# Moving the 8-head attention's value products to other PSUM banks and re-timing a four-layer kernel

## The reference

```python
x = L0(x)  # batchnorm, 3x3 depthwise + 1x1 conv to q,k,v; k,v resized to 7x7; 4-head attention with a bias;
           # 3x3 depthwise + 1x1 conv; + x; batchnorm, relu, 1x1 conv; + residue
x = L1(x)  # group norm; softmax(k) over channels, softmax(q) over pixels; k^T v; q (k^T v); 1x1 conv; + normed x
x = L2(x)  # group norm; qkv; 8 heads of 32 channels: softmax(q^T k / sqrt(32)) v; 1x1 conv; + x
x = L3(x)  # group norm; one head of 256 channels: softmax(q^T k / 16) v; 1x1 conv; + x
```

## Time and profile before

| what | value |
|---|---|
| median of 3 runs | 2110.89 us (2110.83 to 2111.57) |
| the profiled execution | 2112.12 us |
| its span, first to last instruction | 2109.7 us |
| mean granted TensorE clock | 0.98 |
| PE busy | 2011.4 us, 95% |
| ACT busy | 1886.4 us, 89% |
| DVE busy | 1843.0 us, 87% |
| POOL busy | 973.3 us, 46% |

### The profile page before, as it was taken

The page is one execution under the profiler, slowest core; times in us unless marked ns, Lnnn a source line. Parts: engine busy times, 40 slices in busy tenths (PEclk is TensorE's granted clock), DMA queues, the critical chain, the costliest instruction groups (busy, mean ns, idle before and its releaser), DMA issues.

```text
span 2109.7 us, 57712 instructions
## 1 busy us (share of the span) xinstructions
PE 2011.4 (95%) x15232; PEld 1689.6 (80%) x15232; DVE 1843.0 (87%) x4683; ACT 1886.4 (89%) x6231; POOL 973.3 (46%) x1707
## 2 busy tenths in 40 slices
PE   4589999999999999999999999999999999999977
PEld 3367888888888888888888888888888888888766
DVE  6789999999999999999999999999999999997532
ACT  2269999999999999999999999999999999999984
POOL 3544544545444454544445454444545544453211
PEclk8799999999999999999999999999999999999988
DMA  4000011001101100110111011011101101000000
GB/s 129 16 24 24 17 40 40 24 30 38 38 23 38 38 30 24 38 38 23 38 38 36 18 38 38 23 38 38 38 15 38 38 27 34 31 32 17 24 24 39
DMA packets 29819, 70.31 MB, mean 33 GB/s; under 512 B 6252, under 2 KB 7088, under 8 KB 29744
## 3 DMA queue, kind: packets, MB, share of 16 engines
q1 hardware_dynamic: 26928, 67.68, 9.1%
q10 hardware_dynamic: 2816, 1.72, 0.3%
HBM read 30.85 MB, written 12.85 MB: 21 GB/s over the span
## 4 chain that ended last, share of the span: by engine, by line
PE 88%; ACT 4%; DVE 1%; issue 1%; DVEq 0%; ACTq 0%
PE ps_e L1167 21%; PE ps_c L1167 21%; PE ps_b L1167 15%; PE ps_a L1167 11%; PE ps_s L1167 10%; PE ps_s L1222 8%; ACT e L830 1%; PE ps_a L1469 1%; ACT e L822 1%; ACT pt L836 0%; PE ps_e L1298 0%; PE ps_a L1298 0%; DVE nm L958 0%; ACT e L877 0%; ACT kv L742 0%
## 5 line engine op out<-in xcount | busy, mean ns | idle before, releaser
L822 ACT ACTIVATE e<-ps_s,nm 98x196 f32<-98x196 f32 x1024 | 423.9, 436 | 36.2 <-DVE nm L958 32.0
L830 ACT ACTIVATE e<-e,rden 98x196 f32<-98x196 f32 x1024 | 403.2, 462 | 0.2 <-DVE rden L1063 0.2
L1159 DVE SCALAR_TENSOR_TENSOR y<-opad,w_dw,y 128x406 f32<-128x406 f32 x512 | 314.9, 666 | 0.0
L1140 DVE SCALAR_TENSOR_TENSOR y<-xpad,w_dw,y 128x406 f32<-128x406 f32 x512 | 298.4, 636 | 0.0
L587 POOL TENSOR_SCALAR xn<-x,gn_scale,gn_shift 128x196 f32<-128x196 f32 x384 | 286.1, 757 | 20.8 <-POOL gn_shift L582 20.8
L575 POOL TENSOR_TENSOR gn_t<-gn_group 128x4 f32<-128x4 f32 x96 | 27.7, 289 | 563.7 <-DVE gn_group L1008 430.1
L958 DVE TENSOR_REDUCE nm<-ps_s 98x4 f32<-98x784 f32 x256 | 239.4, 966 | 34.2 <-PE ps_s L1167 34.2
L836 ACT COPY pt<-ps_s 98x392 f32<-98x392 f32 x512 | 233.3, 502 | 4.7 <-PE ps_s L1222 2.8
L1222 PE MATMUL ps_s<-w_eye,e 98*98 98x98 f32 x2048 | 228.9, 249 | 7.3 <-ACT e L830 7.2
L1222 PEld LDWEIGHTS ps_s<-w_eye,e 98*98 98x98 f32 x2048 | 200.5, 130 | 38.8 <-issue 22.3
L822 ACT ACTIVATION_READ_ACCUMULATOR e<-ps_s,nm 98x1 f32 x1024 | 222.7, 217 | 0.0
(11 more groups left out here) (223 smaller groups left out, 5326.6 us busy)
## 6 DMA issues: line engine op xcount, KB each, us to landing
x_in<-in_x SPq DMA_DIRECT2D x32, 392.0 KB, 3.2
x_res<-in_x SPq DMA_DIRECT2D x32, 392.0 KB, 3.1
x2b<-x SPq DMA_DIRECT2D x32, 392.0 KB, 2.7
out<-x SPq DMA_DIRECT2D x32, 392.0 KB, 2.6
out_pairs<-out SPq DMA_DIRECT2D x32, 392.0 KB, 2.5
w_q<-in_q SPq DMA_DIRECT2D x3, 256.0 KB
w_k<-in_k SPq DMA_DIRECT2D x3, 256.0 KB
w_v<-in_v SPq DMA_DIRECT2D x3, 256.0 KB
```

The costliest lines, as they stand in the source:

```text
L822: s.activation(e2[:, j, tc], tile(use)[0:HALF, of_image(tc)], ACT.Exp, bias=nm2[:, j, tc:tc + 1], accum_out=den2[:, 2 * i + tc, h:h + 1]). ...
L830: s.activation(e2[:, j, tc], e2[:, j, tc], ACT.Copy, scale=rden2[:, 2 * i + tc, h:h + 1]).then_inc(p2_done[j].sem, 1)
L1140: v.scalar_tensor_tensor(out=dst, in0=window(xpad, c, k, CR), scalar=tap, in1=dst, op0=ALU.mult, op1=ALU.add).then_inc(conv1_steps.sem, 1)
L1159: v.scalar_tensor_tensor(out=dst, in0=window(opad, c, k, CR), scalar=tap, in1=dst, op0=ALU.mult, op1=ALU.add).then_inc(conv2_steps.sem, 1)
```

## The change

The value products leave bank 0 of `ps_s` and go to plain banks: `av0` to e, `av1` to a, `av2` and `av3` to b. All other uses of the plain banks are dealt out anew. The order of the steps on PE, ACT and DVE changes throughout. POOL's order (gn3, gn2, probs0, probs1, rows3, gn1, resize0, resize1) and SP's table stay; two of POOL's numbers change. No instruction of a step is changed, added or removed, except that a value product now waits for the copies of all four `tn{g}_j` where it waited for three of them and for its bank.

In PE's turn after, by place: o3_1, o3_0, tn2_1, tn2_2, tn2_3, tn2_0, v3_1, k0, gn2, **sc3, av2**, s0_0, s0_1, q3_0, mlp1, v3_2, q3_1, tn3_0, v3_3, mlp0, hk0, hq0, t0_0, tn3_3, tn3_1, tn3_2, v3_0, v0, gn1, **sc0, av3**, t0_1, s3_0, o0_1, proj1, o0_0, s3_1, hv0, hk1, hv1, tn0_3, tn0_0, tn0_1, tn0_2, hq1, proj0, **sc1**, kv0, kv1, kv2, t3_0, **av0**, kv3, q0_1, q1_1, q1_0, gn3, tn1_1, tn1_0, tn1_3, tn1_2, ctx0, ctx1, **sc2, av1**, out0, t3_1, out1, q0_0, pw0, pw1.

The diff, cut: of the tables of ACT and DVE only the lines of the steps spoken of below are left.

```diff
 PE_AT = {
-    "q0_1": 102, "q0_0": 115, "k0": 133, "s0_0": 144, "s0_1": 153, "v0": 176, "t0_0": 178, "t0_1": 180, "o0_1": 185,
-    "o0_0": 187, "pw0": 254, "pw1": 268, "mlp0": 283, "mlp1": 284, "gn1": 302, "kv0": 340, "kv1": 342, "kv2": 346,
-    "kv3": 349, "q1_0": 353, "q1_1": 356, "ctx0": 365, "ctx1": 367, "out0": 374, "out1": 376, "gn2": 385, "hk0": 425,
-    "hq0": 429, "sc0": 438, "hv1": 445, "hv0": 448, "tn0_1": 452, "hq1": 454, "tn0_0": 456, "tn0_2": 457,
-    "tn0_3": 461, "hk1": 463, "sc1": 466, "av0": 472, "tn1_1": 483, "tn1_3": 488, "tn1_0": 490, "tn1_2": 492,
-    "sc2": 497, "av1": 506, "tn2_1": 512, "tn2_2": 515, "tn2_3": 519, "tn2_0": 521, "sc3": 526, "av2": 533,
-    "tn3_1": 548, "tn3_0": 549, "tn3_2": 551, "tn3_3": 555, "av3": 575, "proj1": 587, "proj0": 593, "gn3": 607,
-    "q3_1": 658, "v3_1": 659, "v3_2": 663, "q3_0": 670, "v3_0": 672, "v3_3": 674, "s3_0": 695, "s3_1": 706,
-    "t3_0": 731, "t3_1": 757, "o3_1": 764, "o3_0": 778,
+    "q0_1": 99, "q0_0": 122, "k0": 143, "s0_0": 156, "s0_1": 157, "t0_0": 168, "v0": 181, "t0_1": 191, "o0_1": 193,
+    "o0_0": 195, "pw0": 251, "pw1": 254, "mlp1": 287, "mlp0": 293, "gn1": 313, "kv0": 339, "kv1": 340, "kv2": 351,
+    "kv3": 354, "q1_1": 356, "q1_0": 361, "ctx0": 369, "ctx1": 370, "out0": 375, "out1": 377, "gn2": 407, "hk0": 422,
+    "hq0": 423, "sc0": 442, "hv0": 454, "hk1": 455, "hv1": 456, "tn0_3": 458, "tn0_0": 459, "tn0_1": 462,
+    "tn0_2": 463, "hq1": 464, "sc1": 466, "av0": 481, "tn1_1": 493, "tn1_0": 494, "tn1_3": 495, "tn1_2": 496,
+    "sc2": 501, "av1": 502, "tn2_1": 516, "tn2_2": 517, "tn2_3": 520, "tn2_0": 524, "sc3": 536, "av2": 538,
+    "tn3_0": 546, "tn3_3": 553, "tn3_1": 554, "tn3_2": 558, "av3": 574, "proj1": 578, "proj0": 593, "gn3": 620,
+    "v3_1": 653, "q3_0": 670, "v3_2": 672, "q3_1": 673, "v3_3": 675, "v3_0": 692, "s3_0": 704, "s3_1": 709,
+    "t3_0": 736, "t3_1": 760, "o3_1": 770, "o3_0": 771,
 }
...
 ACT_AT = {
...
-    "bn0": 9, "bn1": 12, "q0_1": 121, "q0_0": 130, "k0": 147, "exp0_0": 158, "exp0_1": 166, "t0_0": 184, "v0": 185,
-    "keys2": 365, "keys3": 368, "q1_0": 369, "q1_1": 370, "ctx0": 375, "ctx1": 379, "high2_0": 424, "high2_1": 427,
-    "hk1": 467, "hv0": 470, "sc1_0": 473, "sc1_1": 475, "sc1_2": 476, "sc1_3": 477, "less1_0": 481, "less1_1": 482,
-    "av0": 483, "less1_3": 484, "less1_2": 492, "tn1_3": 494, "tn1_1": 499, "tn1_2": 500, "tn1_0": 502, "sc2_1": 508,
+    "bn0": -33, "bn1": -13, "q0_1": 112, "q0_0": 137, "k0": 162, "exp0_0": 174, "exp0_1": 175, "t0_0": 191, "v0": 192,
+    "keys2": 372, "keys3": 376, "q1_0": 377, "q1_1": 378, "ctx0": 380, "ctx1": 381, "high2_0": 433, "high2_1": 435,
+    "less1_0": 492, "less1_3": 494, "less1_2": 495, "tn1_1": 501, "tn1_0": 502, "tn1_3": 503, "tn1_2": 507,
...
 }
...
 DVE_AT = {
...
-    "conv1_7": 62, "conv1_8": 70, "s0_0": 149, "s0_1": 159, "sum0_0": 160, "sum0_1": 165, "conv2_0": 196,
-    "conv2_8": 252, "pw0": 260, "pw1": 274, "act0_low0": 279, "act0_low1": 284, "mlp0": 290, "mlp1": 296,
-    "max2_0": 502, "max2_1": 504, "rden2_0": 507, "rden2_1": 513, "av1": 519, "max3_0": 532, "max3_1": 536,
+    "conv1_7": 62, "conv1_8": 68, "s0_0": 150, "s0_1": 152, "sum0_0": 155, "sum0_1": 162, "conv2_0": 192,
+    "conv2_8": 255, "pw0": 261, "pw1": 264, "act0_low0": 270, "act0_low1": 273, "mlp1": 281, "mlp0": 297,
+    "max2_0": 501, "max2_1": 504, "rden2_0": 507, "rden2_1": 514, "av1": 519, "max3_0": 528, "max3_1": 532,
...
 }
...
 POOL_AT = {
-    "resize0": 96, "resize1": 112, "probs0": 160, "probs1": 176, "gn1": 336, "gn2": 400, "gn3": 640, "rows3": 704,
+    "resize0": 96, "resize1": 112, "probs0": 148, "probs1": 151, "gn1": 336, "gn2": 400, "gn3": 640, "rows3": 704,
 }
 
 BANK_USES = {
-    "a": ("t0_1", "o0_1", "gn1", "ctx0", "hv0", "gn3", "v3_2", "v3_0", "t3_0", "t3_1", "o3_1",),
-    "b": ("k0", "v0", "o0_0", "mlp0", "q1_0", "ctx1", "out1", "v3_1", "v3_3", "s3_1",),
-    "c": ("q0_0", "s0_0", "pw0", "kv1", "kv3", "q1_1", "hq0", "hq1", "hk1", "q3_0", "s3_0", "o3_0",),
-    "e": ("q0_1", "s0_1", "t0_0", "pw1", "mlp1", "kv0", "kv2", "out0", "gn2", "hk0", "hv1", "proj1",
-          "proj0", "q3_1",),
+    "a": ("k0", "s0_1", "t0_1", "kv3", "q1_0", "hk0", "hv0", "av1", "proj1", "v3_2", "v3_0",),
+    "b": ("q0_1", "q0_0", "t0_0", "o0_1", "mlp0", "kv1", "ctx1", "out0", "av2", "av3", "v3_1", "s3_1", "t3_0", "o3_1",),
+    "c": ("pw1", "gn1", "kv2", "q1_1", "out1", "gn2", "hq0", "hv1", "proj0", "q3_0", "q3_1", "s3_0",),
+    "e": ("s0_0", "v0", "o0_0", "pw0", "mlp1", "kv0", "ctx0", "hk1", "hq1", "av0", "gn3", "v3_3", "t3_1", "o3_0",),
 }
 LAST_LAG = max(max(at.values()) for at in (SP_AT, PE_AT, ACT_AT, DVE_AT, POOL_AT)) // SLOTS
 
@@ -290,8 +289,7 @@
                  for b in "abce"}
         bank_s = [Bank(f"bank_s{j}", ps_s[:, j], [
             use for g in range(GROUPS) for use in (
-                (f"sc{g}_{j}", PE_AT[f"sc{g}"], 2), (f"tn{g}_{j}", PE_AT[f"tn{g}_{j}"], 1),
-                *([(f"av{g}", PE_AT[f"av{g}"], 1)] if j == 0 else []))]) for j in range(HG)]
+                (f"sc{g}_{j}", PE_AT[f"sc{g}"], 2), (f"tn{g}_{j}", PE_AT[f"tn{g}_{j}"], 1))]) for j in range(HG)]
         home = {use: bank for bank in (*banks.values(), *bank_s) for use in bank.lag}
 
         def tile(use):
```

## The result

The changed kernel takes **2122.12 us** in the median (2120.66 to 2124.68, 5 runs), the kernel before 2110.83 in the same runs. The ratio is 1.0055, 95% interval 1.0044 to 1.0067: slower by 11.3 us, where 14 us less were forecast. The profiled execution took 2123.8 us, its span is 2121.8 (before 2112.1 and 2109.7).

What follows compares the result with a forecast made beforehand. PE was taken to set the turn, with ACT 2.7 us behind. Gross savings of 1.1 us less new waits of 0.6 gave 0.5 a turn, 14 us over 28 turns: 2097 us, range 2078 to 2112.

Steps and rivals of the forecast that it cites:

- point 5: New waits per turn: v3_2 behind s0_1 0.4 us, sc2 behind tn1_2 0.2 us, 0.6 in all.
- Point 1: Value products right behind scores (sc3 av2, sc0 av3, sc2 av1): three seams at 0.18, 0.54 us a turn saved.
- 0.80 between starts: Expected sign in the new profile: sc3 followed by av2 with 0.80 us between their starts.
- Point 2: gn2 and gn1 right ahead of sc3 and sc0, one seam instead of two, twice: 0.30 us a turn saved.
- Point 4: Transposes less scattered and gn3 standing elsewhere on PE: 0.1 us a turn saved, between 0 and 0.2.
- point 3: sc2's wait for the copy of tn1_0, behind ctx1 on PE, goes: 0.16 us a turn saved.
- Point 6: No cost from semaphores, banks or other engines' orders: POOL keeps its order and is half idle; lost cover up to 0.3.
- Fill and drain as they are (within 3 us): Start and end of the kernel, where PE isn't the limit, stay unchanged within 3 us.
- The slower one: Rival: ACT's late copies at ctx1 and sc2 delay its next round, 2119 at 1.0 us waiting, 2133 at 1.5; chance 0.15.
- The first rival: All of the gross saving on PE comes through, 1.1 us a turn over 28 turns: 2080 us; chance 0.25.

Runs made afterwards that it cites:

- e2: The changed kernel with v3_2 moved from bank a to c and q3_1 from c to a: 2124.01 us, ratio 1.0056.
- e4: The changed kernel with POOL's probs1 moved behind rows3: 2112.13 us, ratio 1.0007.
- e14: e9 with DVE's run from av2 to mlp0 reordered, ACT's high2_0, q3_1, high2_1, v3_2 reordered, and DVE's mlp0 ahead of sum0_1, av0 ahead of conv2_2: 2100.21 us.
- e10: e9 with one pair taken apart on PE, sc0, t0_1, av3 instead of sc0, av3, t0_1: 2118.42 us, ratio 1.0035.
- e1: The changed kernel with DVE's sum0_1 moved behind low2_0 and low2_1: 2113.74 us, ratio 1.0009.
- e6: The changed kernel with ACT's bn0 and bn1 put back to where they stood before the change: 2119.00 us, ratio 1.0037.
- e9: The changed kernel with e2's swap, e6's bn0 and bn1, DVE's sum0_1 behind low2_1 and rden3_1, ACT's tn1_2 ahead of q1_0 and q1_1: 2113.44 us.
- e12: e4 with e2's swap, e6's bn0 and bn1, e9's ACT order, PE's t0_1 one step later, o0_0 and o0_1 exchanged in order and banks: 2139.77 us.

## Why the prediction was wrong

**What held** is the sum of the savings on PE. It can be had back from the turn, which is 0.30 longer. The new waits, each as its step's excess over the same step in a run that has no such wait, are `v3_2` 0.28 (e2), `hk0` 0.54 (e4), `sc2` 0.24 (e14), `gn3` 0.16 with the step ahead of it (e14) and `o0_1` 0.09 (e4): 1.3 in all, so 1.0 was saved, forecast 1.1. e14 says the same from the other side: 0.61 under the turn before, with waits of 0.32 at `out0` and 0.1 at `o0_1`. Of the waits in point 5, `v3_2` was forecast at 0.4 and is 0.28, `sc2` at 0.2 and is 0.24.

The parts of that sum are shown less well, and it came out in part by luck. Point 1: `sc3` and `av2` keep 0.85 and 0.81; the seam between `sc0` and `av3` is worth 0.15 (e10), and the rows around the other two give about 0.1 and 0.2, some 0.5 of the forecast 0.54. The "0.80 between starts" of my list forgot `sc3`'s own first load, which stays. Point 2 was too high: `gn1` cost 0.13, with 0.09 in `v0` behind it and 0.09 in `t0_1` ahead of `sc0`, 0.31 in all, and costs 0.22 now; `gn2` cost 0.17, with 0.09 in `pw1` ahead of `sc3`, and costs 0.24. That is 0.1 saved of the 0.30. Point 4 was not there: the sixteen `tn` take 5.1 us a turn before and 5.2 after. With point 3's 0.16, some 0.2 of the 1.0 have no place in my list. Steps far from any score or value also change by up to 0.1 with the steps beside them (`v3_3` takes 0.71 before and 0.77 now, `mlp0` 1.17 and 1.08), so the twins from which point 1 read its 0.08 and 0.10 were not neutral.

**What failed is point 5**, "what is late next". I followed DVE from `max3_0` to `s0_1`, because bank a ties `v3_2` to it, found 0.4 us, and stopped. But the run goes on without a gap: `mlp1`, `av2`, two sums, two low halves, 9.7 us in all, and `hk0` comes 9.6 us after `sc3` in the new order. What it takes to see this was at hand: DVE's order in the new table, and the durations of the same operations in the trace of before. With `probs1` out of the way, the run ends 1043.06 + 1.14 - 1034.09 = 10.1 us after `sc3` (e4); `hk0`'s last two matmuls, which read the low halves, are due 9.6 + 4 x 0.18 = 10.3 us after it. A margin of 0.2 us, with `v3_2`'s wait already counted, was the thing to see: any stretch in the run beyond it is a wait. And the two waits are no sum of independent terms, since both end the same run: e2 shows that taking one away adds to the other. By terms: forecast a net of 0.5 saved; less 0.54 at `hk0`, which the sum had at nothing, less 0.25 at `o0_1` and `gn3`, less 0.1 of the gross, and 0.1 more for the smaller wait at `v3_2`: that is -0.3, the measured turn.

**Point 6 failed too**: "POOL keeps its order and is half idle". It keeps its order, but `probs0` and `probs1` moved against DVE's. Before, `low2_0` had begun when `probs1` did, and `low2_1` met only the last 0.3 us of it (0.73 us); now `low2_1` begins while `probs1` has most of its time ahead, and is 1.20 us long. These 0.5 us are more than the whole loss of the turn: e4 takes them away, gives 0.26 back at `t0_1`, and is at 61.35, with before at 61.33. The point cited the exclusive port of the Trainium skill, "SBUF — State Buffer", for POOL's operations only. Its are weaker support than it says: that operation of 3.04 us ends 0.06 us after the last of four taps of DVE, but begins 0.7 us before the first.

The Trainium skill, "SBUF — State Buffer", section "SBUF: two separate sides", says that of a DVE operation with two SBUF inputs and a GpSimd operation that reads SBUF, whichever starts first holds the shared port pair for its whole instruction, and the other fully blocks. The traces agree, either way round. Where POOL was first, DVE lost: 1.26 us in e1, 1.20 in the changed kernel, where `low2_1` ends 0.42 us after `probs1`, against 0.55 without a POOL operation beside it. Where DVE was first, POOL lost: `probs1` of the kernel before took 1.22 us instead of 0.85.

**"Fill and drain as they are (within 3 us)" failed**: +5.1 and +2.3, with 2.8 back in the last three pairs, so some 4.6 in all. The largest part of the fill, 2.9 us by the trace of e6, is a bank shared by two steps that have 14 others between them in the turn and none at the start; it was not mended by itself. What makes the drain longer was not tried.

**The rivals.** None of them was it. The slower one had the right kind of sign and the wrong engine: ACT's late copies at `ctx1` and `sc2` cost the 0.2 of the forecast and no more. That 2122 lies between its 2119 and 2133 is chance. The first rival, all of the gross, is what e14 comes near to (60.72 against 60.2), after several edits to the timetable.

## What to carry to other kernels

When in the steady part PE is busy to nearly 100% and DVE and ACT to 93 and 95%, as here before the change, a saving on PE is worth only what the next engine's run leaves. Take every step of PE that follows an unbroken run of another engine started by PE itself, and add that run up to its end, in the order of the new table, stretching each DVE operation with two SBUF inputs by any GpSimd operation that will run beside it. Waits that end the same run are one wait; mend them in the order of the run, look at the trace after each, and expect a bundle of four edits to hide one that harms.

## What the runs showed of the hardware

- A DVE `tensor_tensor` with two inputs in SBUF (128x392) takes 0.55 us alone (e14), 0.67 to 0.80 when it meets the end of a GpSimd `tensor_tensor` (98x392, 0.85 us alone), and 1.26 when that one began 0.01 us ahead of it (e1). If the DVE operation is first by as little, it takes 0.57 and the GpSimd operation 1.28 (e9). The kernel's time moved by 10 us (0.5%) for one such meeting a turn.
- Leaving a step of 32-row tiles straight for one of 32-column tiles costs what leaving it for full tiles costs in its own tail (`sc0` takes 0.85 for 0.66 us of work in e9 and in e10); what is saved is the entry of the second, 0.15 us in place (e10 against e9).
- A step that waits in an in-order engine's program delays work that has nothing to do with it: by the trace `t0_1`'s copy on ACT, for which ACT stood 1.5 us, cost e12 0.9 us a turn at `s3_1`.
